# Four transformer layers in one launch: the conditioning of one layer in front, that of the others among the first steps, and the last layer's residual sums on VectorE

## The reference

```python
tp = (silu(time_emb) @ Wt + bt)[:, None, :]
shift_msa, scale_msa, gate_msa, shift_mlp, scale_mlp, gate_mlp = split(tp, 6, axis=-1)
h = layernorm(x, g1, be1) * (1.0 + scale_msa) + shift_msa
x = x + gate_msa * attention(h, Wqkv, bqkv, Wproj, bproj)
h = layernorm(x, g2, be2) * (1.0 + scale_mlp) + shift_mlp
x = x + gate_mlp * (gelu(h @ W1 + b1) @ W2 + b2)
```

## Time and profile before

| | |
|---|---|
| median of 3 runs | 2264.01 us (2261.25 to 2267.37) |
| the profiled execution | 2262.32 us, its span 2260.4 us |
| PE busy | 2155.1 us (95% of the span) |
| DVE busy | 1697.4 us (75%) |
| ACT busy | 1249.8 us (55%) |
| POOL busy | 1086.4 us (48%) |
| chain that ended last | PE 84%, DVE 6%, issue 3%, SP's queue 2% |
| mean granted TensorE clock | 0.98 |

### The profile page before, as it was taken

One profiled execution on the slowest core, in us unless ns is written; L12 is line 12 of the kernel. 1 busy time (PEld: TensorE's weight loads), 2 busy tenths in 40 slices (PEclk: granted clock), 3 DMA queues, 4 the chain that ended last, 5 costly groups with the idle time before them and its releaser, 6 DMA issues.

```text
span 2260.4 us, 63283 instructions
## 1 busy us (share of the span) xinstructions
PE 2155.1 (95%) x20080; PEld 1807.2 (80%) x20080; DVE 1697.4 (75%) x4339; ACT 1249.8 (55%) x2618; POOL 1086.4 (48%) x1333
## 2 busy tenths in 40 slices
PE   4699999999999999999999999999999999999997
PEld 2488888888888888888878888888778888787877
DVE  2677777777776777677778777777788888888873
ACT  1366666666565555555676666666654454435441
POOL 2244455455544454445454554446454545444434
PEclk7799999999999999999999999999999999999998
DMA  5422112222222112212331122222222121111210
GB/s 194 131 72 73 63 63 68 70 71 77 85 91 71 62 60 70 74 61 81 102 99 64 60 69 75 66 63 74 86 72 73 55 67 58 63 60 61 65 58 15
DMA packets 164671, 166.11 MB, mean 73 GB/s; under 512 B 29296, under 2 KB 143856, under 8 KB 164560
## 3 DMA queue, kind: packets, MB, share of 16 engines
q1 hardware_dynamic: 164560, 164.69, 22.7%
HBM read 58.47 MB, written 4.39 MB: 28 GB/s over the span
## 4 chain that ended last, share of the span: by engine, by line
PE 84%; DVE 6%; issue 3%; SPq 2%; ACT 1%; POOL 1%; DMA 1%; POOLq 0%; ACTq 0%; DVEq 0%
PE B L530 36%; PE B L630 14%; PE B L799 10%; PE B L776 7%; PE B L577 7%; PE B L639 4%; PE B L649 2%; PE B L733 2%; DVE NEGM L1018 2%; SPq L1407 2%; PE B L554 2%; DVE G L1025 1%; ACT PR L944 1%; ACT G L912 0%; POOL GHl L1300 0%
## 5 line engine op out<-in xcount | busy, mean ns | idle before, releaser
L944 ACT ACTIVATE PR<-B 128x512 f32<-128x512 f32 (+1 forms) x1024 | 504.9, 570 | 282.8 <-PE B L776 280.1
L1300 POOL TENSOR_TENSOR GHl<-G,GHh 128x256 fp32r<-128x256 f32 x512 | 377.6, 738 | 475.2 <-ACT GHh L918 288.4
L1018 DVE TENSOR_REDUCE NEGM<-B 128x2 f32<-128x512 f32 x768 | 485.0, 683 | 91.9 <-PE B L577 91.9
L530 PE MATMUL B<-H2h,W1h 128*128 128x256 f32 x1280 | 397.8, 311 | 3.1 <-issue 3.1
L530 PE MATMUL B<-H2h,W1l 128*128 128x256 f32 x1280 | 363.2, 284 | 0.0
L530 PE MATMUL B<-H2l,W1h 128*128 128x256 f32 x1280 | 362.7, 283 | 0.0
L918 ACT ACTIVATE G<-B,VEC 128x256 f32<-128x256 f32 x384 | 182.0, 474 | 284.2 <-PE B L530 284.2
L630 PE MATMUL B<-W2h,GHh 128*128 128x256 f32 x1024 | 297.1, 290 | 1.7 <-POOL GHl L1300 1.7
L630 PE MATMUL B<-W2l,GHh 128*128 128x256 f32 x1024 | 290.3, 283 | 0.0
L630 PE MATMUL B<-W2h,GHl 128*128 128x256 f32 x1024 | 289.6, 283 | 0.0
L530 PEld LDWEIGHTS B<-H2h,W1h 128*128 128x128 f32 x1280 | 244.3, 191 | 44.4 <-issue 26.4
(11 more groups left out here) (160 smaller groups left out, 4704.1 us busy)
## 6 DMA issues: line engine op xcount, KB each, us to landing
QS<-QHL SPq DMA_DIRECT2D x768, 64.0 KB, 2.1
KS<-KHL SPq DMA_DIRECT2D x768, 64.0 KB, 2.1
GA<-gate_scratch SPq DMA_DIRECT2D x48, 256.0 KB, 3.2
GM<-gate_scratch SPq DMA_DIRECT2D x48, 256.0 KB, 3.4
RAW<-in_w SPq DMA_DIRECT2D x36, 256.0 KB, 3.5
CW<-in_cw SPq DMA_DIRECT2D x3, 1536.0 KB, 12.4
QS<-MT SPq DMA_DIRECT2D x256, 4.0 KB
GA<-in_rows_last SPq DMA_DIRECT2D x16, 256.0 KB, 3.3
```

What stands on the lines that cost most here:

```text
L530: last = nc.tensor.matmul(dst, w[i], x[j], start=(first_k and n == 0), stop=(last_k and n == 2))
L944: nc.scalar.activation(PR[:, h % PRING].rearrange("p k q -> p (k q)")[:, 0:n], src[:, 0:n], ACT.Exp, scale=SCALE).then_inc(ac_exp, 1)
L1018: last = nc.vector.tensor_reduce(NEGM[:, :, c], src, op=ALU.max, axis=AX.X, negate=True)
L1300: nc.gpsimd.tensor_tensor(GH[1][:, j % RING, :], G[:, j % RING, :], GH[0][:, j % RING, :].bitcast(F32), ALU.subtract).then_inc(po_gl, 1)
```

## The change

The block in front and its barrier are gone. Only layer 0's modulation and gates are computed before the first step; POOL's memsets and the load and split of `EQ` stand beside it. Layer 1's modulation and layer 3's first product come at the end of step -1, layer 3's second product and layer 2's modulation in the middle of step 0, each engine's part at a place of its own. The matrices lie in tiles that are idle at that time: layer 0's in PR, layers 1 and 2's in the places of sequences 2 to 13 of X, layer 3's in those of sequences 14 and 15 and in PR, `EQ` in G and GK, `EO` in OR, gate rows in TOK, OR and GM. So x is loaded later: two sequences in front, two in step 0, the other twelve (3 MB, before eight of them, 2 MB, at the end of step -1) at the end of step 0. The gate rows go to DRAM in step 0 by six DMAs, and SP waits for their landing there. The plan of layer 0's MLP weights moves by about half a step.

In layer 3 DVE adds the projection's and the MLP's results from PSUM directly to x (`add_to_x`); POOL's two sums go, its bias sums come earlier (j == 1 and j == 3), `statistics_2` moves to j == 5, POOL's `rstd` ahead, and `normalise_2` stands ahead of the rotation. The store of a tile waits for DVE instead of POOL.

```diff
-        plan = {(0, EARLY): part(0, "1", 0, 2), (0, LATE): part(0, "2", 0, 1),
-                (1, EARLY): part(0, "1", 1, 3), (1, LATE): part(0, "2", 2, 3)}
+        plan = {(0, LATE): part(0, "1", 0, 2), (1, EARLY): part(0, "2", 0, 1),
+                (1, LATE): part(0, "1", 1, 3), (2, FIRST): part(0, "2", 2, 3)}
...
+        CW_ALL = [words(PR)[:, 0:CWN], sequences(2, 8), sequences(8, 14)]
...
+        CT1 = sequences(14, 16).rearrange("p (k n) -> p k n", k=KD)
+        CT2 = words(PR)[:, 0:KD * 4 * D].rearrange("p (k n) -> p k n", k=KD)
+        EQ = [words(w)[:, 0:WQ_COLS[0]] for w in (G, GK)]
...
+            def gates(l):
+
+                for k in range(KD):
+                    for r, c0 in enumerate((2 * D, 5 * D)):
+                        last = nc.tensor.matmul(B[gate_part(r), GATE_BANK[l], 0:D], SC[:, k, 0:NSEQ], CW[l][k][:, c0:c0 + D],
+                                                start=(k == 0), stop=(k == KD - 1))
+                last.then_inc(pe_gates, 1)
...
+            modulation(0)
+            gates(0)
+            modulation_to_features(0)
+
             def body(s):
...
                     if p == 0:
                         at_least(pe, ac_exp, H * s.na)
+                    if p < 2 and isinstance(a_, int) and a_ == 0:
+                        pe.wait_ge(dv_cond, 2)
+                        pe.wait_ge(dv_t1, KD)
+                        pe.wait_ge(dv_rows, 4)
...
                 down_if(4)
+                if isinstance(s.a, int) and s.a == 0:
+                    modulation(ROPE)
+                    modulation_to_features(ROPE)
+                    modulation(2)
+                    gates(2)
+                    modulation_to_features(2)
                 scores_if(4)
                 scores_if(5)
                 if scored:
                     maxima_to_rows(0)
                 up_if(7)
                 down_if(5, 6)
+                if isinstance(s.a, int) and s.a == 0:
+                    pe.wait_ge(dv_cond, NL)
+                    pe.wait_ge(dv_rows, 6)
...
+                if isinstance(s.q, int) and s.q == 0:
+                    conditioning()
+                    modulation(1)
+                    pe.wait_ge(dv_cond, 1)
+                    gates(1)
+                    modulation_to_features(1)
             steps(pe, body)
...
                     if j == 4:
                         if s.q is not None:
                             normalise_1(s.q, s.sq, s.lq, s.nq)
+                        if isinstance(s.q, int) and s.q == 0:
+                            first_modulation()
                         if s.r is not None:
                             dv.wait_ge(pe_wo, s.r + 1)
-                            multiply(s, bank(WO_BANK), GA, sp_ga, s.r, s.lr).then_inc(dv_wo, 1)
+                            if s.lr == ROPE:
+                                add_to_x(s.sr, po_xb1, s.r, bank(WO_BANK)).then_inc(dv_wo, 1)
+                            else:
+                                multiply(bank(WO_BANK), GA, sp_ga, s.r).then_inc(dv_wo, 1)
                         maxima(2)
                     if j == 5:
                         maxima(3)
+                        if isinstance(s.a, int) and s.a == 0:
+                            modulation(ROPE)
+                            modulation(2)
+                            gate_rows(2)
+                        if s.lr == ROPE:
+                            statistics_2()
...
-                statistics_2()
+                if s.lr != ROPE:
+                    statistics_2()
                 if s.lq == ROPE:
                     r = s.q - NSEQ * ROPE
+                    if s.lr == ROPE:
+                        normalise_2()
                     rotate(s, pe_q, 1, G, V_BQ, V_BQR, 0)
...
+                if isinstance(s.q, int) and s.q == 0:
+                    gate_rows(0)
+                    modulation(1)
+                    condition()
+                    gate_rows(1)
+
+            def add_to_x(sequence, s_bias, n, src):
+                x = X[:, seq(sequence), :, :].rearrange("p a t d -> p (a t) d")
+                dv.wait_ge(s_bias, n + 1)
+                apart(dv)
+                return nc.vector.tensor_tensor(x, x, src, ALU.add)
...
-                    if j == 4 and s.r is not None:
+                    if j == (1 if s.lr == ROPE else 4) and s.r is not None:
                         residual_1_bias(s)
-                    if j == 5 and s.r is not None:
+                    if j == 3 and s.lm == ROPE:
+                        residual_2_bias(s)
+                    if j == 5 and s.r is not None and s.lr != ROPE:
                         residual_1(s)
...
             def store(s, tile, sequence):
-                hold(po_x2, tile + 1)
+                hold(dv_dn, tile + 1)
...
                     if isinstance(s.a, int) and s.a == 0:
-                        sp.wait_ge(sp_gs, 16)
+                        gate_scratch()
...
                     if isinstance(s.q, int) and s.q == 0:
-                        sp.dma_start(X[:, 8:16], a["x"].rearrange("s (t p) d -> p s t d", p=P)[:, 8:16]).then_inc(sp_x[2], 16)
                         sp.wait_ge(sp_const, 48)
+                    elif isinstance(s.q, int) and s.q == 1:
+                        sp.dma_start(X[:, 4:16], x_in[:, 4:16]).then_inc(sp_x[2], 16)
...
+            def gate_scratch():
+                sp.wait_ge(dv_rows, 6)
+                for r in range(2):
+                    for l in range(NL - 1):
+                        sp.dma_start(g_scr[l, :, 2 * r:2 * r + 2, :], GR[l][gate_part(r)]).then_inc(sp_gs, 16)
+                sp.wait_ge(pe_gates, NL - 1)
+                sp.dma_start(X[:, 2:4], x_in[:, 2:4]).then_inc(sp_x[1], 16)
+                sp.wait_ge(sp_gs, 96)
+
+            sp.dma_start(CT[:], a["c_t"]).then_inc(sp_ct, 16)
+            sp.dma_start(X[:, 0:2], x_in[:, 0:2]).then_inc(sp_x[0], 16)
+            modulation_in(0)
+            sp.dma_start(VEC[:], a["vec"]).then_inc(sp_cw[0], 16)
+            sp.dma_start(IDENT[:], a["ident"]).then_inc(sp_cw[0], 16)
+            sp.wait_ge(sp_x[0], 16)
+            for k in range(KD):
+                sp.dma_start(EQ[k], a["wq0"][k * P:(k + 1) * P, :]).then_inc(sp_first[0], 16)
+            sp.wait_ge(sp_cw[0], 80)
+            sp.dma_start(CT1, a["cw_t1"].rearrange("(k p) n -> p k n", p=P)).then_inc(sp_t1, 16)
+            modulation_in(1)
+            sp.dma_start(EO, a["wo0"].rearrange("(k p) n -> p k n", p=P)).then_inc(sp_first[1], 16)
+            modulation_in(2)
+            sp.wait_ge(pe_gates, 1)
+            sp.dma_start(CT2, a["cw_t2"].rearrange("(k p) n -> p k n", p=P)).then_inc(sp_t2, 16)
...
```

More of the change, by code:

```diff
@@ L456, in build, with words, sequences @@
         W1 = [sb(f"W1{x}", [P, KD, 2 * DFF], F32R) for x in "hl"]
         W2 = [sb(f"W2{x}", [P, NJ, D], F32R) for x in "hl"]
+        def words(tile):
+            flat = tile[:].bitcast(F32)
+            return flat.rearrange("p a b -> p (a b)") if len(tile.shape) == 3 else flat.rearrange("p a b c -> p (a b c)")
+        def sequences(first, last):
+            return X[:, first:last, :, :].rearrange("p s t d -> p (s t d)")
+        CWN = KD * 6 * D
+        CW_ALL = [words(PR)[:, 0:CWN], sequences(2, 8), sequences(8, 14)]
@@ L460, in build, with gate_part @@
+        LAYERS = (0, 1, ROPE, 2)
+        def gate_part(r):
+            return slice(32 * r, 32 * r + NSEQ)
+        starts = [(D, 0, 4 * D, 3 * D)] * 3 + [(D, 0, 3 * D, 2 * D)]
         class Step:
@@ L541, in weights @@
             def weights(l, what, first_tile, *which):
-                if not (isinstance(first_tile, int) and first_tile == 0) or (l == 0 and what in "qo"):
+                if not (isinstance(first_tile, int) and first_tile == 0):
+                    return
+                if l == 0 and what == "q":
+                    pe.wait_ge(ac_first, KD)
+                    pe.wait_ge(dv_first, 1)
+                    pe.wait_ge(po_first, 1)
+                    return
+                if l == 0 and what == "o":
+                    pe.wait_ge(po_first, 2)
                     return
@@ new lines, in first_modulation @@
+            def first_modulation():
+                dv.wait_ge(sp_cw[0], 80)
+                chain(nc.vector.tensor_scalar(SCP[:], VEC[:, :, 0:8].rearrange("p l (h x f) -> p l h x f", h=2, x=2)[:, :, :, 0, :],
+                                              1.0, None, ALU.add))
+                settle()
+                modulation(0)
+                dv.wait_ge(ac_first, 1)
+                nc.vector.tensor_tensor(WQ[0][1][:, 0, :], EQ[0], WQ[0][0][:, 0, :].bitcast(F32),
+                                        ALU.subtract).then_inc(dv_first, 1)
@@ L1195, in body, with multiply @@
                     evacuate(1)
-            def multiply(s, src, rows, s_rows, n, layer):
-                if layer == ROPE:
-                    return nc.vector.tensor_copy(TOK[:], src)
+                if isinstance(s.q, int) and s.q == 0:
+                    gate_rows(0)
```

(6 more changed lines are left out.)

347 lines of the change are left out of this document (162 added, 185 removed).

## The result

The changed kernel takes 2235.4 us (median of four runs, 2234.2 to 2237.3) against 2262.6 (2259.3 to 2267.4) before: ratio 0.9877, 95% interval 0.9858 to 0.9896. The profiled execution took 2234.2 us with a span of 2231.9, 28.5 us less than the 2260.4 of before; by the medians it is 27.2, where the forecast had 30.

A forecast was written before the change was run, and what follows sets the result against it. PE, 84% of the chain that ended last, was taken to bound the kernel. Start -18.2, layer 3 -7.5 and drain -4.4 sum to -30.1 us: 2232.2 against the profiled execution, so 2234 as median; range 2223 to 2249.

The forecast's parts named there:

- First query product: Start: PE's first query product comes at 20.1 us, 31.9 us earlier, bounds 29 and 34.
- What returns: Steps -1 and 0: the modulation work moved there gives back 8.9 us, bounds 5 and 12.
- 5 (PE at its full clock): Steps -1 and 0: lower bound of 5 us returned, if modulation and gates take half at PE's full clock.
- Load of x: Step 1: PE waits 4.8 us for MT behind the 3 MB load of x, bounds 0 and 7.
- Rival 1: Step 1: the 4.8 us wait leaves PE at the lower clock for half the dense stretch, +7 us, 2241; chance 0.17.
- Net of the start: Start through step 1: -31.9 + 8.9 + 4.8 = -18.2 us.
- rival 3: Start cheaper: MT passes the load of x, or PE runs new products at full clock; 5 to 8 less, 2228; chance 0.15.
- Layer 3: Steps 49 to 62: PE's wait at outputs(2) falls from 0.72 to 0.2 us, -7.5 us in all, bounds -1 and -10.
- Rival 2: Layer 3: the gap is ACT's, so nothing is won there, 2241.5 us; chance 0.12.
- Drain: Step 64 and end: second norm 3.0 us earlier, POOL's sum of 1.35 gone, -4.4 us, bounds -3 to -7.
- Rivals 4 and 5: 4: POOL's earlier bias sums delay PE's down, 2278, chance 0.03. 5: modulations stay on the path, 2247, chance 0.04.

The follow-up runs named there:

- e8: Changed kernel with x of sequences 4 to 15 in three 1 MB loads spread over steps 0 and 1: 2229.9 us, ratio 0.9855.
- e11: Changed kernel with layer 3's second-norm statistics, reciprocal root and norm in their old order, sums on DVE and early bias sums kept: 2237.2 us, ratio 0.9896.
- e5: Changed kernel with the second norm behind the rotation, as before, in step 49 alone: 2232.4 us, ratio 0.9870.
- e4: Changed kernel with PE's second-norm transposes ahead of transposed pairs 4 and 5 in layer 3: 2237.7 us, ratio 0.9887.
- e6: Changed kernel with layer 3's second product made twice by PE in step 0: 2236.2 us, one run.
- e7: Changed kernel with layer 3's first product made twice by PE in step -1: 2238.5 us, one run.
- e10: Changed kernel with x in three spread loads, step 49's second norm behind the rotation, and layer 3's second half of the values ahead of outputs(2): 2220.4 us, ratio 0.9807.
- e9: Changed kernel with PE's second half of the values ahead of outputs(2) in layer 3: 2229.2 us, ratio 0.9850.
- e2: Changed kernel with layer 3 as it was before, so the new start alone: 2241.0 us, ratio 0.9899.
- e3: Changed kernel with x of sequences 4 to 15 in three 1 MB loads at the ends of steps 0, 1 and 2: 2242.0 us, ratio 0.9899.

## Why the prediction was right, and where it was not

**First query product: predicted 20.1, measured 18.77.** The mechanism was right; three sizes were off. The matrix released PE at 10.19 and not 11.1: the half megabyte of x in front of it did not show, for up to 10 us the queue moved 0.3 MB more than before (175 GB/s in the first 5 us against 119, then 377 against 371). The gates took 1.95, not 1.7. ACT's two copies of EQ ended at 13.34, not 14.8 (which the prediction's own terms, 14.13 + 1.4 - 0.5, would have at 15.0). So POOL's split ended at 15.23, not 16.6; COND's product, beside it, ended at 15.31, and its last operation at 15.70, not 17.1. From HF to the query it was 2.97 again. Gain 33.3 in place of 31.9.

**What returns: predicted 8.9, measured 5.5** (54.00 against the 81.74 of the earlier trace rows, less 33.3). The failed step is a size that the prediction had as its bound "5 (PE at its full clock)": conditioning, modulation and gates of step -1 took 1.85, 1.07 and 1.03 us, together 4.0, where 3.60, 1.94 and 1.7 were summed. The durations of the earlier trace rows are from a stretch in which PE was half idle (the 3.60 follows on 6.67 us of waiting, granted clock 0.50); in their new place they follow directly on 6.7 us of query products (18.77 to 25.47), at 1.00. Step 0's products did take what was summed (1.94 each, gates 1.83). What came behind was right: from the first scores to maxima(4) 15.3 us predicted, 15.3 measured (33.22 to 48.47), and 5.6 to the pairs, measured 5.5. SP was free in time for the second row of maxima.

**Load of x: predicted 4.8, measured 3.6 of wait and 4.3 in all** (e8). From the load's issue to PE's release it is 13.1 us, by the prediction's steps 13.2. Rival 1, that the wait leaves PE at the lower clock for 7 us, came true in its mechanism (granted clock 0.61 from 75 to 90 us, 0.95 from 90 to 112), at a tenth of its price, if the 0.7 left of e8's gain are its.

**Net of the start: predicted -18.2, measured -23.0.** That is the second condition of rival 3, PE at full clock in new products, at nearly its price.

**Layer 3: predicted -7.5, measured about -0.3.** Three steps failed. First, the wait was expected to fall from 0.72 to 0.2 with HF beginning as the transposes end; it fell to 0.42, since HF starts 0.28 us behind the end that the profile gives them. The statistics' move is so worth 0.29 us a step (e11), not 0.52. Second, "add_to_x costs what the copy did" holds for its duration and not for its place: with the earlier bias sums it costs 0.18 a step (e11). Left are 0.11 a step, 1.3 us in twelve steps. Third, step 49 was counted like the others (-0.8); there the norm, moved ahead, waits for POOL's sum of layer 2, and the step lost 1.5 us (e5). Step 62 gave another 0.5. Rival 2 has nearly the right gain in layer 3 (nothing) for the wrong reason: the gap was HF's and not ACT's, as e11's rows show, although e4 shows that ACT is next.

**Drain: predicted -4.4, measured -3.9**, in the terms named: 1.41 us of idle PE ahead of the second norm (4.42 in the earlier trace rows), and POOL's sum gone:

```profile
2204.41 0.66 PE L537 MATMUL B<-IDENT,TOK 128*128 128x128 f32 x4 [1.41 <-DVE TOK L931]
...
2228.57 0.69 DVE L1232 TENSOR_TENSOR X<-X,B 128x512 f32<-128x512 f32 x1 [2.03 <-PE B L528]
```

**The rest.** Another 1.2 us were won between steps 32 and 49, which nothing in the prediction covers. Nearly all of it is step 33, in which weights of the next layer's MLP are split: PE waits there for DVE's product with a gate, 2.08 us before and 0.99 in the changed kernel. DVE stands behind ACT's split of the weights W2, and ACT behind their landing, first before, then changed:

```profile
1157.29 0.63 ACT L253 ACTIVATE W2h<-RAW 128x512 fp32r<-128x512 f32 x1 [0.79 <-DMA RAW<-in_w]
...
1133.18 0.64 ACT L253 ACTIVATE W2h<-RAW 128x512 fp32r<-128x512 f32 x1 [0.19 <-DMA RAW<-in_w]
```

Of the kernels with the new start some have the short wait there (1.0 us in e6, e7, e10 and e11, 1.2 in e5 and e9), others the long one (1.9 in e2, e3, e4 and e8), so I put it down to chance and not to the change; why the landing differs was not looked for. Step 17 has such a wait too: 1.1 us in most of the executions, 2.1 in e3 and e9, 2.9 in e7. Rivals 4 and 5 did not come: no wait of PE for a low half of the hidden part stands in layer 3, and the modulations did leave the path.

So the total was right by luck, through two errors that offset: 4.8 us too little for the start, 7.2 too much for layer 3. The larger part, that the modulations leave PE's path, was no luck.

## What to carry to other kernels

A duration read in a half idle stretch is not the duration in its new place: for a moved PE product ask at which clock its new neighbours run. When one wait has several releasers nearly abreast, moving one of them earlier wins only up to the next; filling the wait with independent work of the waiting engine won all of it here. The name in a wait's row is then no proof: set the end of each candidate beside the moment at which the engine went on. An edit that is right in the steady steps must be read once more in the steps where a layer changes, and one long load is better cut and spread than put ahead of a small transfer that an engine waits for.

## What the runs showed of the hardware

A long load also holds the queue's issuing engine: SP's two issues of RAW took 6.06 us behind 3 MB, 2.45 behind 2 MB (the kernel before), 1.05 and 1.99 behind 1 MB (e8, two places) and 0.95 with no load ahead. TensorE's clock makes executions differ: the same 16 products took 1.07 us in e2 and 1.94 in the changed kernel, with 40 us of the same instructions in front, and behind the doubled product of e6 they took 1.07 again. Across the kernels that share this start, step 2 began from 1.8 us earlier (e2, where the rows show the clock as the reason) to 1.3 later (e9, not followed up) than in the changed kernel. When a weight load lands differs as well, and moved PE by 1 us in step 33.
